# A decoder layer in split fp32: gate and up as block products of seven multiplications

## What is computed

```
h2 = rmsnorm(x1, ln2_w)                        # 1024 tokens x 512
x2 = x1 + (silu(h2 @ gate_w.T) * (h2 @ up_w.T)) @ down_w.T
```

## Time and profile before

| | |
|---|---|
| median of 3 runs | 428.29 us (428.06 to 430.07) |
| the profiled execution | 430.06 us, its span 428.0 us |
| granted clock of TensorE, mean | 0.999 of full speed |
| TensorE busy | 414.6 us, 97% of the span |
| VectorE, ScalarE, GpSimd busy | 206.5, 162.9, 67.3 us |
| moved by DMA | 25.4 MB, mean 59 GB/s |

### The profile page before, as it was taken

The page is one execution under the profiler, slowest core; times in us unless marked ns, Lnnn a source line. Parts: engine busy times, 40 slices in busy tenths (PEclk is TensorE's granted clock), DMA queues, the critical chain, the costliest instruction groups (busy, mean ns, idle before and its releaser), DMA issues.

```text
span 428.0 us, 5201 instructions
## 1 busy us (share of the span) xinstructions
PE 414.6 (97%) x1908; PEld 328.0 (77%) x1912; DVE 206.5 (48%) x390; ACT 162.9 (38%) x332; POOL 67.3 (16%) x53
## 2 busy tenths in 40 slices
PE   7999999999989999999999999999999999999984
PEld 3878887666658888888888888888787887887762
DVE  2496991246574331313131313153455675676566
ACT  5668733845732422222222222343133133232231
POOL 3403213533571302020202010100000000000000
PEclk9999999999999999999999999999999999999999
DMA  7601111110020030303031312111100211201001
GB/s 258 235 2 50 51 49 49 50 49 2 1 98 2 7 127 15 129 18 114 33 106 41 100 47 98 49 49 51 49 21 29 74 31 44 74 25 50 26 0 74
DMA packets 10114, 25.41 MB, mean 59 GB/s; under 512 B 1681, under 2 KB 1809, under 8 KB 10098
## 3 DMA queue, kind: packets, MB, share of 16 engines
q1 hardware_dynamic: 8946, 23.10, 16.4%
q10 hardware_dynamic: 1152, 2.10, 1.3%
HBM read 23.10 MB, written 2.10 MB: 59 GB/s over the span
## 4 chain that ended last, share of the span: by engine, by line
PE 91%; DVE 5%; ACT 2%; issue 1%; ACTq 0%; DVEq 0%
PE bank L369 25%; PE bank L371 24%; PE bank L370 24%; PE bank L440 2%; PE bank L427 2%; PE bank L487 2%; PE bank L588 2%; PE bank L577 1%; PE bank L380 1%; PE bank L599 1%; PE bank L449 1%; PE bank L408 1%; DVE tmp L1172 1%; PE bank L470 1%; PE bank L569 1%
## 5 line engine op out<-in xcount | busy, mean ns | idle before, releaser
L369 PE MATMUL bank<-cols,ringS 128*128 128x512 f32 x304 | 119.5, 393 | 1.3 <-DVE cols L1009 1.3
L371 PE MATMUL bank<-cols,ringS 128*128 128x512 f32 x304 | 118.4, 389 | 0.0
L370 PE MATMUL bank<-cols,ringS 128*128 128x512 f32 x304 | 118.3, 389 | 0.0
L1139 DVE TENSOR_TENSOR big<-tmp,bank 128x512 f32 (+1 forms) x28 | 19.3, 688 | 103.0 <-ACT tmp L872 103.0
L369 PEld LDWEIGHTS bank<-cols,ringS 128*128 128x128 f32 x304 | 57.1, 188 | 14.2 <-issue 2.6
L370 PEld LDWEIGHTS bank<-cols,ringS 128*128 128x128 f32 x304 | 57.1, 188 | 12.1 <-issue 0.5
L371 PEld LDWEIGHTS bank<-cols,ringS 128*128 128x128 f32 x304 | 57.1, 188 | 12.0
L369 PE MATMUL bank<-wdS,cols 128*128 128x512 f32 x144 | 61.4, 427 | 0.0
L872 ACT ACTIVATE tmp<-bank 128x512 f32<-128x512 f32 x28 | 16.8, 598 | 105.6 <-PE bank L371 105.6
L371 PE MATMUL bank<-wdS,cols 128*128 128x512 f32 x144 | 56.4, 392 | 0.0
L370 PE MATMUL bank<-wdS,cols 128*128 128x512 f32 x144 | 56.2, 390 | 0.0
(11 more groups left out here) (142 smaller groups left out, 518.9 us busy)
## 6 DMA issues: line engine op xcount, KB each, us to landing
raw<-wstream SPq DMA_DIRECT2D x31, 512.0 KB, 3.3
rows<-x SPq DMA_DIRECT2D x8, 256.0 KB, 5.0
big<-ctxT SPq DMA_DIRECT2D x8, 256.0 KB, 2.6
big<-ctx SPq DMA_DIRECT2D x8, 256.0 KB, 2.9
out<-tmp ACTq DMA_DIRECT2D x8, 256.0 KB, 2.0
big<-ln_w SPq DMA_DIRECT2D x1, 256.0 KB, 5.5
big<-lora_b SPq DMA_DIRECT2D x3, 64.0 KB, 4.7
ga<-gate_lora SPq DMA_DIRECT2D x1, 72.0 KB, 5.3
```

Of the source, the lines that this page charges most:

```text
L369: pe.matmul(ps, a_hi, b_lo, start=first, stop=False)
L370: pe.matmul(ps, a_hi, b_hi, start=False, stop=False)
L371: return pe.matmul(ps, a_lo, b_hi, start=False, stop=last)
L1139: v.tensor_tensor(dst, blocks(hn[:, par, :]), blocks(bank[4 * par + 2 * hf + 1][:, :]), ALU.mult) \
```

## The change

Pair 0 stays as it was. For pairs 1 to 6 the gate blocks (2j, 2j + 1) and the up blocks are each a group, g = 2 to 13, even for gate, odd for up. A group is a product of 2 x 2 blocks: A (two output blocks x two halves of the 512 features) times B (two halves of the features x two halves of the tokens). It is made with seven multiplications (Winograd's form) of 128 outputs x 256 features x 512 tokens: 7 x 2 chunks x 3 passes = 42 matmuls. The products go through all eight PSUM banks in turn.

- Sums of B: T1 to T4 are made once from h2, by token blocks 4 to 7, in fp32: on VectorE `token_sums` (six instructions of 128 x 256), on GpSimd `t3_rest` (one of 128 x 256); then high part on ScalarE (`hi_of_t`, 128 x 1024), low part on GpSimd (`t_low`). Their fp32 scratch `tf` is one and the same for tokens 4, 5 and 7.
- Sums of A: S1 to S4 per group, four instructions of 128 x 256 on GpSimd (`weight_sums`), high part on ScalarE (128 x 1024), low parts on VectorE (2 x 128 x 512); of the blocks themselves 128 x 512 and 128 x 256 (`weight_hi`, `weight_lo`).
- Sums of products: one copy on ScalarE (P1) and seven `combine` of 128 x 512 on VectorE per group, each with a PSUM input; then four silus on ScalarE (even groups), and three up products on GpSimd and one on VectorE (odd groups), with both inputs in SBUF.
- h2 of tokens 4 to 7 is written in two pieces. The memory of h2 and the T's (`moving`, 7 x 2 x 1024 columns) is later that of w_down: its piece j takes the place of the moving operand of product j, so the split of w_down is moved to the end of the last group and the first down tile (pieces 0, 2, 4: low part on GpSimd, the others on VectorE). `raw` has four buffers for three; y gets its own buffers. SP's loads follow: one of 512 KB per group (two rows of 2 KB for one of 4 KB), then w_down's seven, then two of the base weight, which are split behind tile 1's hidden values (`bw_high`, `bw_low`) in the place where the last pair did it.
- TensorE gets waits: `t_step` before the classic products of pair 0 that overwrite the banks from which `token_sums` reads, `t_lo` before the first group's second product, `g_lo`, `consumed`, and the pieces of w_down in the first tile.

The diff, cut (blank lines left out):

```diff
-RAW = 3
+RAW = 4
...
+PRODUCTS = ((A11, B11), (S2, T2), (S1, T1), (S3, T3), (S4, B22), (A22, T4), (A12, B21))
+P1, P6, P5, P7, P3, P4, P2 = range(7)
+WD_SET = tuple(moving for _, moving in PRODUCTS)
...
+POOL_WD = (0, 2, 4)
...
...
+        part1 = (tmp[:, 4 * D:5 * D], tmp[:, 5 * D:6 * D])
...
+        tf = (tmp[:, 4 * D:6 * D], tmp[:, 4 * D:6 * D], side[:, 2 * D:4 * D], tmp[:, 4 * D:6 * D])
...
+                elif n - RAW < LOOP_CHUNK:
+                    sp.wait_ge(gu_done, 4)
+                    sp.wait_ge(t3_ok, HB)
...
+                    wait_wd_lo(sp, j - RAW)
+                sp.dma_start(raw[:, raw_slot(n), :], wstream[LOOP_CHUNK + 3 * j]).then_inc(raw_in[raw_slot(n)], 16)
...
+                wait_wd_lo(sp, NM // 2 - RAW + i)
+                sp.dma_start(raw[:, raw_slot(n), :], wstream[LOOP_CHUNK + 3 * (NM // 2 - 1) + 1 + i]) \
...
+            def t_low(t):
+                pool.wait_ge(t_hi, t - HB + 1)
+                pool.tensor_tensor(t_cols(t, 1), t_f32_of(t), t_cols(t, 0).bitcast(F32), ALU.subtract).then_inc(t_lo, 1)
+            def t3_rest(t):
+                f = t_f32_of(t)[:, 2, :, :]
+                pool.wait_ge(t_diff, t - HB + 1)
+                pool.tensor_tensor(f, f, b12S[:, 1, :, bass.ts(t - HB, P)].bitcast(F32), ALU.subtract).then_inc(t3_ok, 1)
...
+            def weight_sums(g):
...
+                pool.wait_ge(raw_in[raw_slot(n)], landed(n))
...
+                else:
+                    pool.wait_ge(g_lo, 4 * i)
+                pool.tensor_tensor(s1, a21, a22, ALU.add).then_inc(g_sum, 1)
+                pool.tensor_tensor(s3, a11, a21, ALU.subtract).then_inc(g_sum, 1)
+                pool.wait_ge(g_sum, 4 * i + 1)
+                pool.tensor_tensor(s2, s1, a11, ALU.subtract).then_inc(g_sum, 1)
+                pool.wait_ge(g_sum, 4 * i + 3)
+                pool.tensor_tensor(s4, a12, s2, ALU.subtract).then_inc(g_sum, 1)
...
+            def wd_low(j):
+                n = wd_load(j)
+                pool.wait_ge(wd_hi, j + 1)
+                pool.tensor_tensor(wdS[:, WD_SET[j], 1, :], raw[:, raw_slot(n), :],
+                                   wdS[:, WD_SET[j], 0, :].bitcast(F32), ALU.subtract).then_inc(wd_lo2, 1)
+            t3_rest(HB)
+            t_low(HB)
+            t3_rest(HB + 1)
+            t_low(HB + 1)
+            weight_sums(G0)
+            t3_rest(HB + 2)
+            t_low(HB + 2)
+            t3_rest(HB + 3)
+            t_low(HB + 3)
+            for g in range(G0, N_GROUP):
+                if g + 1 < N_GROUP:
+                    weight_sums(g + 1)
+                else:
+                    wd_low(POOL_WD[0])
+                if g % 2 == 1:
+                    up_product(g, 3, st_c22, c22[1])
+                    up_product(g, 1, st_c12, u4[1])
+                    if g < N_GROUP - 1:
+                        up_product(g, 2, st_c21, u2u3[1])
+            wd_low(POOL_WD[1])
...
+            def strassen(g):
...
+                for n, (a, m) in enumerate(PRODUCTS):
+                    q = 7 * i + n
+                    if n == 0:
+                        pe.wait_ge(g_lo, 4 * i + 2)
+                    if n == 1:
+                        pe.wait_ge(g_lo, 4 * i + 4)
+                        if i == 0:
+                            pe.wait_ge(t_lo, HB)
+                    if q < 8:
+                        pe.wait_ge(hid_ok, q // 2 + 1)
+                    else:
+                        pe.wait_ge(consumed[(q - 8) % 7], (q - 8) // 7 + 1)
+                    for c in range(2):
+                        w = bass.ds(a * HALF_K + c * P, P)
+                        mm = three_pass(pe, product_bank(g, n), groupS[:, buf, 0, w], groupS[:, buf, 1, w],
+                                        movingS[:, m, 0, c, :], movingS[:, m, 1, c, :], c == 0, c == 1)
+                    mm.then_inc(st_done, 1)
             pe.wait_ge(h2_lo, B - 2)
+            pe.wait_ge(t_step, 3)
             gate_up(1, 0, (0,))
-            turn_h2(B - 2, 6)
-            turn_h2(B - 1, 7)
+            turn_h2(B - 2)
+            turn_h2(B - 1)
+            pe.wait_ge(t_step, 7)
             gate_up(1, 0, (1,))
             pe.wait_ge(h2_lo, B)
             gate_up(0, 1)
+            pe.wait_ge(t_step, 15)
             gate_up(1, 1)
...
+            for g in range(G0, N_GROUP):
+                strassen(g)
...
+                    if first_use:
...
+                        pe.wait_ge(consumed[q % 7], q // 7 + 1)
+                    if first_tile:
+                        pe.wait_ge(hid0_lo, 1)
+                    else:
+                        pe.wait_ge(hid_lo, t + 1)
                     if not first_use:
                         pe.wait_ge(ln_u[0], t - 1)
                 for k in range(k0, k1):
+                    if first_tile and k % 2 == 0:
+                        if k // 2 in POOL_WD:
+                            pe.wait_ge(wd_lo2, POOL_WD.index(k // 2) + 1)
+                        else:
+                            pe.wait_ge(wd_lo, k // 2 - sum(i < k // 2 for i in POOL_WD) + 1)
+                    if first_tile and k == NM - 2:
+                        pe.wait_ge(hid_lo, 1)
...
+            def hi_of_t(t):
+                act.wait_ge(t_f32, t - HB + 1)
+                act.wait_ge(t3_ok, t - HB + 1)
+                act.activation(t_cols(t, 0), t_f32_of(t), ACT.Copy).then_inc(t_hi, 1)
...
+            hi_of_h2(B - 2)
+            hi_of_t(HB)
+            hi_of_h2(B - 1)
+            hi_of_t(HB + 1)
...
+            def weight_hi(g):
...
+                elif i == 1:
+                    act.wait_ge(gu_done, 4)
+                else:
+                    act.wait_ge(st_done, 7 * (i - 1))
+                act.activation(groupS[:, buf, 0, 0:D], raw[:, raw_slot(n), 0:D], ACT.Copy).then_inc(g_hi, 1)
+                act.activation(groupS[:, buf, 0, D:D + HALF_K], raw[:, raw_slot(n), D + HALF_K:2 * D], ACT.Copy) \
...
+            def sums_hi(g):
...
+                act.wait_ge(g_sum, 4 * (i + 1))
+                act.activation(groupS[:, buf, 0, D + HALF_K:7 * HALF_K], sums, ACT.Copy).then_inc(g_hi, 1)
...
+            def copy_p1(g):
...
+                act.wait_ge(st_done, 7 * i + P1 + 1)
+                if i < 2:
+                    act.wait_ge(t_lo, HB)
+                elif buf == 1:
+                    act.wait_ge(up11_ok, i // 2)
+                act.activation(part1[buf], product_bank(g, P1), ACT.Copy).then_inc(st_p1, 1)
...
+            def wd_high(j):
...
+                act.wait_ge(raw_in[raw_slot(n)], landed(n))
+                act.wait_ge(st_done, 7 * (N_GROUP - 1 - G0) + j + 1)
+                act.activation(wdS[:, WD_SET[j], 0, :], raw[:, raw_slot(n), :], ACT.Copy).then_inc(wd_hi, 1)
...
+            sg_classic(0, 0, 0)
+            weight_hi(G0)
+            hi_of_t(HB + 2)
+            sg_classic(1, 1, 0)
+            hi_of_t(HB + 3)
+            sums_hi(G0)
+            sg_classic(2, 0, 1)
+            sg_classic(3, 1, 1)
+            for g in range(G0, N_GROUP):
+                i, buf = g - G0, g % 2
+                last = g == N_GROUP - 1
+                if not last:
+                    weight_hi(g + 1)
+                copy_p1(g)
+                if not last:
+                    sums_hi(g + 1)
+                else:
+                    wd_high(0)
+                    act.wait_ge(st_done, 7 * i)
+                    act.wait_ge(up_ok, 3 * (i // 2))
+                    act.wait_ge(up11_ok, i // 2)
+                    act.activation(hidS[:, 0, 0, 0:(NM - 2) * P], big[:, 0:(NM - 2) * P], ACT.Copy).then_inc(hid0_hi, 1)
+                    for j in range(1, NM // 2 - 1):
+                        wd_high(j)
+                if buf == 0:
+                    gate_silu(g, 3, st_c22, c22[0])
+                    gate_silu(g, 1, st_c12, u4[0])
+                    gate_silu(g, 2, st_c21, u2u3[0])
+                    gate_silu(g, 0, st_c11, part1[0])
+            act.wait_ge(up11_ok, NM // 2 - 1)
+            act.activation(hidS[:, 0, 0, (NM - 2) * P:NM * P], big[:, (NM - 2) * P:NM * P], ACT.Copy).then_inc(hid_hi, 1)
+            wd_high(NM // 2 - 1)
...
+            def token_sums(t):
...
+                if i == 0:
+                    v.wait_ge(h2_ps, t + 1)
+                    v.wait_ge(dec_exp, H * B)
+                if i in (1, 3):
+                    v.wait_ge(t_lo, (1, None, 2)[i - 1])
+                if i == 2:
+                    v.wait_ge(op_done, B)
+                v.tensor_tensor(f[:, 0, :, :], b12, b11[0], ALU.subtract).then_inc(t_step, 1)
+                v.wait_ge(h2_lo, t + 1)
+                v.tensor_tensor(f[:, 2, :, :], b22, b12S[:, 0, :, q].bitcast(F32), ALU.subtract).then_inc(t_diff, 1)
+                v.wait_ge(t_step, 4 * i + 1)
+                v.tensor_tensor(f[:, 0, :, :], f[:, 0, :, :], b11[1], ALU.subtract).then_inc(t_step, 1)
+                v.wait_ge(t_step, 4 * i + 2)
+                v.tensor_tensor(f[:, 1, :, :], b22, f[:, 0, :, :], ALU.subtract).then_inc(t_step, 1)
```

(70 more changed lines are left out.)

325 lines of the change are left out of this document (226 added, 99 removed).

## The result

The changed kernel took 439.91 us (median of 4 executions, 439.59 to 441.2) against 428.83 for the kernel before in the same session: a ratio of 1.026, 95% interval 1.0236 to 1.0284. The forecast was 433.2, slower; the sign is right, the time is off by 6.7 us (11.1 us slower for 4.9 forecast). The profiled execution took 440.2, span 438.2. All lines here are of that one unless another kernel is named; its groups answer to the earlier trace rows.

What follows compares the result with a forecast made beforehand. The kernel was taken as bound by TensorE's count of 512-column matmuls. Terms: -16.3 (72 fewer matmuls) + 13.0 (front) + 0 (loop) + 7.2 (end) = +3.9 on 428.29, 432.2, plus 1 = 433.2 us; range 425.5 to 441.

Steps and rivals of the forecast that it cites:

- First, second and third wait of the front: Before the loop, TensorE waits for token sums: 3.1, 5.6 and 4.2 us; group 2 starts 13.0 us later with restarts.
- the walk: Step-by-step timing of the token-sum chain before the loop on the old trace's clock, giving +13.0 us.
- The end: First down tile: late splits of w_down make TensorE wait 1.1, 2.0 and 3.9 us, +7.2 us with restarts.
- The term of the loop: Groups of 9.52 us in which the added work fits beside TensorE: no added time, possible waits bounded by 5 us.
- I take 0: In the loop, the next group's sums before TensorE's second product were taken to cost nothing.
- the line: Straight-line instruction prices from 512 and 1,024 columns; for GpSimd 1.28 and 2.39 us, giving 0.71 for 256.
- The term of the clock: Clock falling to half behind waits: a rival at 435 to 437 us, chance 0.12; part of 1 us added to the sum.
- the 1 us that the sum added: Added to 432.2 us for the clock and for small errors that can only add lateness, giving 433.2.
- the 3 to 5 of the rival: Clock rival: a fall behind the front's third wait adds 3 to 5 us, giving 435 to 437; chance 0.12.
- A covered end: Rival: down-weight pieces ready when wanted, end costs under 1 us, 425.0 us, faster; chance 0.14.
- two shorter chains: Rival: front 11.6 to 12.5 us and end 3.3 to 5, total 427 to 430; chance 0.23.
- a loop that costs 6 us: Rival: loop bound by VectorE and GpSimd, +0.5 us in each of twelve groups, 438 us; chance 0.15.

Runs made afterwards that it cites:

- the first try with idle matmuls: Changed kernel plus idle matmuls in all three front waits (12, 22, 10) and ahead of pairs 4 and 6 (5, 9) of the first down tile: 439.56 us.
- the repeat: The changed kernel measured once more with no edit: 438.73 us, ratio 1.0217.
- the small shares: Changed kernel with GpSimd's low parts of its three down-block pairs at the end on 32 of 1,024 columns, work left out: 433.78 us, one execution.
- the loop order: Changed kernel with GpSimd forming the next weight sums ahead of its last up product, one group further ahead: 435.85 us, ratio 1.0158.
- small weight sums: Changed kernel with GpSimd's weight sums on 32 of 256 columns from the second group on, work left out: 436.41 us, one execution.
- idle matmuls in the right places: Changed kernel plus idle matmuls in three front waits (12, 22, 10) and ahead of pairs 1, 2, 3 (4, 8, 9) of the first down tile: 437.19 us.
- two parts less: The kernel with all rearrangements together, without the token sums' low parts on VectorE and the early first silu: 426.07 us, ratio 0.9927.
- the end's order: Changed kernel with the new loop order, and GpSimd splitting its three down-block pairs before its last two up products: 434.37 us, ratio 1.014.

## Why the forecast was right in direction and wrong in size

**First, second and third wait of the front: right.** Said 3.1, 5.6 and 4.2 us, measured 2.96, 5.25 and 2.41. The places and the causes are those of the walk:
```profile
137.78 1.05 DVE L1427 TENSOR_TENSOR tmp<-tmp,moving 128x256 f32<-128x256 f32 x1
```
This third instruction of the first token's sums took 1.05 us instead of 0.42 behind GpSimd's residual, the high and low part of token 4 stood in the second, the table load, the weight parts and sg_classic(1) in the third. The third is shorter because the fall of the clock behind the second (12 matmuls at 0.427) was absorbed by it; from the second to the third waited matmul it was 12.87 us in this profile, 12.86 in others with a shorter fall, and 12.90 in the two with idle matmuls and no fall there. Without the fall the third wait was 4.4, as the first try with idle matmuls shows. Without falls the front is 42.7 - 29.3 = 13.4 us longer, for 13.0.

**The end: right in cause and place, its exact size partly luck.** Said 1.1, 2.0 and 3.9, measured 1.32, 2.34 and 2.56, and in the repeat 1.35, 1.81 and 3.70. Without a fall 16.7 - 9.5 = 7.2 us, for 7.2; in the repeat 18.9 - 1.6 - 9.5 = 7.8. The single waits were off by up to 1.3 us, both ways. That three of VectorE's instructions stand behind GpSimd's was the reason given, and the small shares show it.

**The term of the loop: wrong, 2.8 us.** The step that failed is "I take 0". The forecast named the right place, the next group's sums behind three up products, and even the waits (0.5 to 0.9 us in every other group, bounded by 5), but only for a GpSimd 5 to 10% slower than the line. It had not walked the chain, whose instructions hold each other. Here GpSimd's timeline, at the start of an odd group's end:
```profile
246.06 4.24 POOL L512 TENSOR_TENSOR big<-tmp,side_f 128x512 f32<-128x512 f32 x3 [4.20 <-DVE side_f L1495]
250.27 1.18 POOL L499 TENSOR_TENSOR side_f<-raw 128x256 f32<-128x256 f32 x1
251.42 1.18 POOL L500 TENSOR_TENSOR side_f<-raw 128x256 f32<-128x256 f32 x1
```
Three products in 4.24 us instead of 3 x 1.28, then two sums of 1.18 instead of 0.74 (the line from 512 and 1,024 columns had said 0.71). Moving the sums ahead of one product, and one group further ahead, took the whole term away. Holding did not make the loop bound by VectorE and GpSimd, as the rival had it: the same work fits, in another order.

**The term of the clock: wrong, 4.4 us in the profiled execution** (2.8 in the first wait, 1.6 at the end), for part of the 1 us that the sum added. The step that failed is the sentence that a fall behind the second wait is free and one behind the third costs up to 5.4. Its first half is right, and a fall behind the third, where one came, cost 1.6 and not the 3 to 5 of the rival. It left out the end, though the same rival counts 3.7 us of standstill there, and the first wait, 3 us long, which I had not taken for long enough since the longest old gap, 1.34 us, had no fall behind it, and the earlier trace rows shows 4.3 us at 1.00 after the last matmul. A row at the end of a kernel said nothing on a pause between bursts. The rule in "TensorE: Matmul & The Clock Gate" of the Trainium skill (Why this matters for your kernels), that pauses between bursts halve the clock, agrees with this trace (0.50 behind the first wait), though the same 2.96 us passed without a fall in other executions (the last section). I had given that outcome 435 to 437 and 0.12, as a rival to the forecast; it was a term that came on top of it, and so did the loop's, as neither excludes the other. With both: 433.2 - 1 + 2.8 + 4.4 = 439.4, measured 439.91, and 438.73 in the repeat.

**The rivals.** A covered end and two shorter chains did not occur, nor did a loop that costs 6 us. The range to 441 held.

## What to carry to other kernels

Price a cut in matmuls together with what its preparation puts in front of TensorE: here 16.3 us were saved, 20.6 lost in two short stretches with pauses, 2.8 in the loop, and 4.4 more in the clock behind the pauses. Add up small terms that can all occur; a list of rivals with one chance each hides their sum. Where two engines hold each other, the order on the slower one can be worth as much as its load: moving one block of sums brought the loop to the 114.24 us that leaving most of the sums out gave, and moving two products brought the end to what small shares gave (8.1 and 8.2 us to the last wait's end). The change became a gain (0.9899) by arrangement alone.

## What was not expected of the hardware

- The same wait of 2.96 us met a clock that fell 2.1 us after TensorE had stopped (the changed kernel), 4.3 us after it (its repeat), or not at all (the loop order, whose front is the same). From the first to the second waited matmul it took 11.9, 10.7 and 9.1 us accordingly. Of the six profiles with this front and no idle matmuls four have such a fall. The slow stretches lasted 3.4 to 6.8 us. What decides is not shown.
- The spread between executions is larger than for the kernel before: 437.1 to 441.2 over ten executions of the changed kernel, 428.0 to 430.4 for the one before, most of them under 428.8. Falls of 0 to 3 in three places account for some of it. In the first try with idle matmuls, 442.86 us at a mean clock of 0.991 is not explained by them, and stays open.
- Four of the profiled executions (the kernel before, small weight sums, idle matmuls in the right places, two parts less) reach the first mark at 125.5 us, the others at 123.4 to 124.3. The table gives these four a granted clock of 1.00 over the whole start, and so the kernel before its mean of 0.999, but that is no reading: TensorE ran slowly there. In the kernel before, four matmuls of 512 columns stand 0.43 us apart at 10.4 us, the pitch behind the falls, and are done in 1.12 us at 13.8. Its transposes, beside those of the kernel with the end's order, whose table also shows 1.00 there and whose first mark is at 123.41:
```profile
8.68 1.94 PE L380 MATMUL bank<-ident,tmp 128*128 128x128 f32 x8 [0.93 <-DVE tmp L1003]
10.41 1.91 PE L487 MATMUL bank<-big 128*128 128x512 bf16 x4
12.12 1.91 PE L380 MATMUL bank<-ident,tmp 128*128 128x128 f32 x8
13.82 1.12 PE L487 MATMUL bank<-big 128*128 128x512 bf16 x4
```
```profile
7.87 1.22 PE L575 MATMUL bank<-ident,tmp 128*128 128x128 f32 x8 [0.93 <-DVE tmp L1298]
8.93 1.03 PE L683 MATMUL bank<-big 128*128 128x512 bf16 x4
```
  So an execution can start 1.2 to 2.1 us late by its clock while its mean clock looks the best of all: the kernel before took 430.05 us at 0.999 and 428.3 at 0.995.
- Idle matmuls are no sure cure: ten in a wait of some 4 us left 2.2 of it, and the clock fell behind it in one kernel (idle matmuls in the right places) and not in the other (the first try), with the same edit in the front.
